# Row products by four blocks, scalings shared with ScalarE, and adjacency loads ahead of a store, in a four-layer graph network

## The reference, cut to what matters

```python
x = _layernorm(x + _L0_gnn_ref(x, ...))      # returns updated + x, so the norm sees 2x + updated
x = _layernorm(x + _L1_gnn_ref(x, ...))
x = _layernorm(x + _L2_gnn_ref(edge_index, x))
x = _layernorm(x + _L3_gnn_ref(x, ...))
```

```python
x_tangent = logmap0(x, c)                     # artanh(|x|) * x / |x|, a factor per row
support = x_tangent @ weight
hyp_bias = proj(expmap0(bias[None, :], c), c)
support = proj(mobius_add(support, hyp_bias, c), c)
agg = segment_sum(edge_weight[:, None] * support[col], row)
return proj(expmap0(agg, c), c)

def mobius_add(x, y, c):
    x2, y2, xy = sum(x * x), sum(y * y), sum(x * y)
    num = (1.0 + 2.0 * c * xy + c * y2) * x + (1.0 - c * x2) * y
    return num / maximum(1.0 + 2.0 * c * xy + c * c * x2 * y2, MIN_NORM)
# proj(x): x scaled down to norm 0.996 where its norm is larger
```

## Time and profile before

| | |
|---|---|
| median of three runs | 5073.99 us (5068.99 to 5074.60) |
| the profiled execution | 5076.37 us, its span 5074.6 us |
| busy: PE, PEld, DVE, ACT, POOL | 3733.3, 2726.1, 3254.3, 1313.6, 1977.1 us |
| accumulation | 2314 to 3121 us |
| first norm and row products, to the end of S | 3121 to 3235 us |
| weighted adjacency | 3235 to 3924 us |
| second norm | 3924 to 3973 us |

### The profile page before, as it was taken

How to read it: one execution, slowest core, us unless ns; L and a number is a source line. 1 busy time by engine, 2 the same in 40 slices (tenths; PEclk the granted TensorE clock), 3 DMA queues, 4 the chain that set the end, 5 groups by cost and what they waited for, 6 DMA issues and landing times. The chain is left out here.

```text
span 5074.6 us, 99492 instructions
## 1 busy us (share of the span) xinstructions
PE 3733.3 (74%) x38930; PEld 2726.1 (54%) x38930; DVE 3254.3 (64%) x4529; ACT 1313.6 (26%) x3164; POOL 1977.1 (39%) x2050
## 2 busy tenths in 40 slices
PE   4457755555555555555888886499998699989997
PEld 3345655555555555545777775255555244444444
DVE  7886898888888889875777766666666400230022
ACT  0015666555565555640000002100001100010000
POOL 0051277777776777745777773000000003000300
PEclk6558898988988889887999997799999899989998
DMA  9636889999999999997788785488885467656664
GB/s 314 225 103 223 274 301 342 337 340 342 342 338 334 338 343 347 339 247 236 228 230 232 226 230 121 183 304 305 304 305 203 152 204 227 198 165 202 212 191 140
DMA packets 710810, 1297.27 MB, mean 256 GB/s; under 512 B 367384, under 2 KB 512428, under 8 KB 701260
## 3 DMA queue, kind: packets, MB, share of 16 engines
q1 hardware_dynamic: 579516, 823.86, 49.9%
q10 hardware_dynamic: 60300, 314.88, 16.2%
q0 software_dynamic: 70576, 152.66, 11.7%
HBM read 814.90 MB, written 529.03 MB: 265 GB/s over the span
## 5 line engine op out<-in xcount | busy, mean ns | idle before, releaser
L1460 PE MATMUL psum<-big 128*128 128x98 bf16 x7936 | 925.7, 215 | 702.5 <-DVE big L1441 489.6
L1411 POOL DMA_INDIRECT big<-typed_msgs,big x1216 | 1150.1, 946 | 516.2 <-issue 330.7
L1460 PEld LDWEIGHTS psum<-big 128*128 128x128 bf16 x7936 | 789.7, 100 | 755.9 <-DVE big L1441 524.6
L2111 PE MATMUL psum<-big 128*128 128x512 bf16 (+1 forms) x4704 | 992.1, 373 | 82.3 <-DMA big<-adj 82.3
L1461 PE MATMUL psum<-big 128*128 128x49 bf16 x7936 | 911.5, 197 | 2.3 <-issue 2.3
L1462 PE MATMUL psum<-big 128*128 128x49 bf16 x7936 | 907.0, 190 | 0.1
L1462 PEld LDWEIGHTS psum<-big 128*128 128x128 bf16 x7936 | 838.0, 106 | 1.7 <-issue 1.6
L1461 PEld LDWEIGHTS psum<-big 128*128 128x128 bf16 x7936 | 794.5, 100 | 2.7 <-issue 2.7
L2111 PEld LDWEIGHTS psum<-big 128*128 128x128 bf16 x4704 | 460.3, 98 | 605.6 <-DMA big<-adj 82.8
L1696 PE MATMUL psum<-big 128*128 128x192 f32 x3648 | 647.5, 333 | 118.2 <-DMA big<-typed_msgs,big 98.0
L1921 PE MATMUL psum<-big 128*128 128x416 f32 x1984 | 655.4, 494 | 63.4 <-DVE big L1955 62.3
(11 more groups left out here) (320 smaller groups left out, 2753.2 us busy)
## 6 DMA issues: line engine op xcount, KB each, us to landing
wadj<-big ACTq DMA_DIRECT2D x248, 784.0 KB
big<-wadj SPq DMA_DIRECT2D x124, 1568.0 KB, 7.0
big<-adj SPq DMA_DIRECT2D x210, 896.0 KB, 4.8
big<-staged SPq DMA_DIRECT2D x304, 384.0 KB
staged<-big SPq DMA_DIRECT2D x60, 1920.0 KB
adj<-big ACTq DMA_DIRECT2D x62, 1568.0 KB
big<-edge_feats SPq DMA_DIRECT2D x456, 128.0 KB
edge_feats<-in_edge_attr SPq DMA_DIRECT2D x1, 51562.5 KB, 162.5
```

Of the source, the lines that this page charges most:

```text
L1411: pool.indirect_dma_start(out=sgot4[:, c, u, 0:D], out_offset=None, in_=typed_rows, in_offset=bass.IndirectOffsetOnAxis(ap=pairs4i[:, g, u ...
L1460: pe.matmul(to[:, 0:2 * NB], lo, hi_b[:, q, t, 0:2, 0:NB], start=True, stop=False)
L2111: last = pe.matmul(ps[c % 2][:, 0:len(blocks) * P], terms_[:, k, b * D:(b + 1) * D], ring_a[:, m % RA, 0:len(blocks), s * P:(s + 1) * P], ...
```

## The change

In the accumulation, the first 128 columns of each block of `acc` start as 2X in place of zero, the other 64 as zero. The pass L1734 is dropped, and the norm reads `acc` in place.

In the row products, ScalarE's copies of X are dropped: TensorE turns four blocks straight from X into one PSUM bank, ScalarE evicts the 512 columns at once, TensorE makes four products into one bank, and ScalarE evicts them at once. TensorE turns the next four blocks ahead of the products of the last. VectorE's sums stay per block, written out in place of a loop.

The norm of the result is computed from the sums at hand (|a s + p y|^2 = a^2 s^2 + 2 a p s y + p^2 y^2), and the factor of `proj` is folded into `a` and `part_y`. Then ScalarE scales blocks 0 to 39 by `a`, VectorE blocks 40 to 48, and VectorE adds the bias part block by block, waiting for ScalarE's block where it is one.

In the weighted adjacency stage the store of `support` is issued after the first four loads. The degree roots move from the second norm to VectorE's list between its last transpose and its last evictions. The squares behind the stage move into it: VectorE makes them block by block behind ScalarE's evictions, and ScalarE's part of them is dropped.

```diff
@@ accumulation, VectorE
-                dve.memset(acc, 0.0).then_inc(s_clear, 1)
+                dve.tensor_scalar(acc3[:, :, 0:D], X3, 2.0, None, ALU.mult).then_inc(s_clear, 1)
+                dve.memset(acc3[:, :, D:ACCW], 0.0).then_inc(s_clear, 1)
@@ first norm, VectorE
-                link(dve.scalar_tensor_tensor(h43, X3, 2.0, sums, ALU.mult, ALU.add))
...
-                layer_norm(dve, link, h43, chain.sqrt, logs)
+                layer_norm(dve, link, sums, chain.sqrt, logs)
...
-                        dve.wait_ge(s_S5, i * BB + (k + 1))
-                        at_least(dve, s_sum5, (i * BB + (k + 1 - BB)) * 2)
...
+                for b in range(NB):
+                    k = b % BB
+                    dve.wait_ge(s_S5, b // BB + 1)
+                    at_least(dve, s_sum5, (b + 1 - BB) * 2)
...
-                link(dve.tensor_tensor(S3, S3, along(a), ALU.mult))
-                link(dve.tensor_tensor(sq43, bias3, along(x2), ALU.mult))
-                link(dve.tensor_tensor(S3, S3, sq43, ALU.add))
-
-                sum_of_squares(dve, link, S3, sq43, den)
-                chain.sqrt(den, a)
-                link(dve.tensor_scalar(a, a, MIN_NORM, None, ALU.max))
-                link(dve.reciprocal(a, a))
-                link(dve.tensor_scalar(a, a, MAX_NORM, 1.0, ALU.mult, ALU.min))
-                link(dve.tensor_tensor(S3, S3, along(a), ALU.mult))
+                link(dve.tensor_tensor(sq, a, x2, ALU.mult))
+                link(dve.tensor_tensor(den, part_y, xy, ALU.mult))
+                link(dve.scalar_tensor_tensor(sq, den, 2.0, sq, ALU.mult, ALU.add))
+                link(dve.tensor_tensor(sq, sq, a, ALU.mult))
+                link(dve.tensor_tensor(den, part_y, part_y, ALU.mult))
+                link(dve.scalar_tensor_tensor(sq, den, y2, sq, ALU.mult, ALU.add))
+                link(dve.tensor_scalar(sq, sq, 0.0, None, ALU.max))
+                chain.sqrt(sq, den)
+                link(dve.tensor_scalar(den, den, MIN_NORM, None, ALU.max))
+                link(dve.reciprocal(den, den))
+                link(dve.tensor_scalar(den, den, MAX_NORM, 1.0, ALU.mult, ALU.min))
+                link(dve.tensor_tensor(a, a, hi, ALU.mult))
+                link(dve.tensor_tensor(a, a, den, ALU.mult))
+                dve.sem_inc(s_factor, 1)
+                link(dve.tensor_tensor(part_y, part_y, den, ALU.mult))
+                for b in range(SCALED, NB):
+                    made = dve.tensor_scalar(S3[:, b, :], S3[:, b, :], a[:, b:b + 1], None, ALU.mult)
+                link(made)
+                for b in range(NB):
+                    if b < SCALED:
+                        dve.wait_ge(s_scaled, b + 1)
+                    made = dve.scalar_tensor_tensor(S3[:, b, :], b1b[:, :], part_y[:, b:b + 1], S3[:, b, :], ALU.mult, ALU.add)
+                link(made)
@@ row products, ScalarE
-                    for k in range(n):
-                        at_least(act, s_xT5, i * BB + (k + 1 - BB))
-                        act.copy(xst4[k], X[:, bass.ds(i * (BB * D) + k * D, D)]).then_inc(s_xs5, 1)
...
+                def rows_out(j):
+                    b0, b1 = QUADS[j]
+                    act.wait_ge(s_o5, j + 1)
+                    act.copy(S[:, b0 * D:b1 * D], ps[BB + j % 4][:, 0:(b1 - b0) * D]).then_inc(s_S5, 1)
+
+                for j, (b0, b1) in enumerate(QUADS):
+                    act.wait_ge(s_xT5, j + 1)
+                    at_least(act, s_o5, j - 1)
+                    act.copy(xTs[:, j % 2, 0:(b1 - b0) * D], ps[j % 4][:, 0:(b1 - b0) * P]).then_inc(s_xTe5, 1)
+                    if j:
+                        rows_out(j - 1)
+                rows_out(len(QUADS) - 1)
                 chain.answer(act, before_products[0])
+                act.wait_ge(s_factor, 1)
+                for b in range(SCALED):
+                    act.activation(S3[:, b, :], S3[:, b, :], ACT.Identity, scale=sm(6)[:, b:b + 1]).then_inc(s_scaled, 1)
@@ row products, TensorE
+                def products(j):
+                    b0, b1 = QUADS[j]
+                    pe.wait_ge(s_xTe5, j + 1)
+                    at_least(pe, s_S5, j - 3)
+                    for i in range(b1 - b0):
+                        last = pe.matmul(ps[BB + j % 4][:, i * D:(i + 1) * D], xTs[:, j % 2, i * D:(i + 1) * D], w1s[:, :],
+                                         start=True, stop=True)
+                    last.then_inc(s_o5, 1)
+
+                for j, (b0, b1) in enumerate(QUADS):
+                    at_least(pe, s_xTe5, j - 3)
+                    for b in range(b0, b1):
+                        last = pe.transpose(ps[j % 4][:, (b - b0) * P:(b - b0 + 1) * P], X[:, b * D:(b + 1) * D], ident)
+                    last.then_inc(s_xT5, 1)
+                    if j:
+                        products(j - 1)
+                products(len(QUADS) - 1)
@@ weighted adjacency, SP
-                sp.dma_start(support.rearrange("(b p) f -> p b f", p=P), S3).then_inc(s_support, 16)
                 for s in range(S2):
                     for m, j in enumerate(blocks7):
                         n = s * GB + m
+                        if n == RW:
+                            sp.dma_start(support.rearrange("(b p) f -> p b f", p=P), S3).then_inc(s_support, 16)
                         at_least(sp, s_turned7, n - RW + 1)
@@ weighted adjacency, VectorE, behind the last transpose; the roots leave the second norm
+                link(dve.tensor_scalar(dinv, outdeg, 1.0, None, ALU.add))
+                chain.sqrt(dinv, dinv)
+                link(dve.reciprocal(dinv, dinv))
+                link(dve.tensor_scalar(degn, indeg, 1.0, None, ALU.max))
+                chain.sqrt(degn, degn)
+                link(dve.reciprocal(degn, degn))
                 take(1)
+                for b in range(NB):
+                    dve.wait_ge(s_agg7, b // QUAD + 1)
+                    row = agg_st[:, b * D:(b + 1) * D]
+                    made = dve.scalar_tensor_tensor(sq83[:, b, :], row, 1.0, row, ALU.mult, ALU.mult, accum_out=sm(3)[:, b:b + 1])
+                link(made)
@@ second norm, VectorE
-                sum_of_squares(dve, link, g, sq83, raw)
```

More of the change, by code:

```diff
@@ L129 @@
 BB = 4
-SHARE = 18
 NORM_SHARE = 19
@@ L659, in wide @@
             return v.rearrange("p (b f) -> p b f", b=NB)
-        def sum_of_squares(dve, link, h3, sq3, to):
-            asked = chain.squares(h3, sq3, to)
-            link(dve.tensor_tensor(sq3[:, SHARE:, :], h3[:, SHARE:, :], h3[:, SHARE:, :], ALU.mult))
-            link(dve.tensor_reduce(out=to[:, SHARE:], in_=sq3[:, SHARE:, :], axis=AX.X, op=ALU.add))
-            dve.wait_ge(chain.did, asked)
         def layer_norm(dve, link, h3, ask_sqrt, before_x=lambda: None, counted=False):
@@ L721, in sqrt @@
                 self.func(ACT.Sqrt, i, o)
-            def squares(self, h3, sq3, to):
-                self.k += 1
-                self.jobs.append((self.k, None, h3, sq3, to))
-                self.dve.sem_inc(self.ask, 1)
-                return self.k
             def rows(self, h3, x3, scale, shift_):
@@ L744, in answer @@
                         made.then_inc(self.did, 1)
-                    elif f is not None:
+                    else:
                         act.activation(o, i, f).then_inc(self.did, 1)
-                    else:
-                        for b in range(SHARE):
-                            made = act.activation(o[:, b, :], i[:, b, :], ACT.Square, accum_out=to[:, b:b + 1])
-                        made.then_inc(self.did, 1)
         s_turn = sem("s_turn")
@@ L1702, in build @@
         sq4, S = (cut(i * NB * D, NB * D)[0] for i in range(2))
-        h4, rest4 = cut(2 * NB * D, NB * D)
+        e_turned, at = cut(2 * NB * D, NB * P)
+        e_turned = e_turned[0:FE, :]
+        xTs, at = cut(at, 2 * BB * D)
+        xTs = xTs.rearrange("p (k x) -> p k x", k=2)
         assert NB * ACCW <= 2 * NB * D
-        h43, S3, sq43 = wide(h4), wide(S), wide(sq4)
-        def staged(n, width):
-            nonlocal rest4
-            c, rest4 = cut(rest4, n * width)
-            return [c[:, k * width:(k + 1) * width] for k in range(n)]
-        xst4, xTs4 = staged(BB, D), staged(BB, D)
-        e_turned = staged(1, NB * P)[0][0:FE, :]
+        S3 = wide(S)
         EB = 4
@@ L1719, in build @@
         s_x1 = sem("s_x1")
-        s_xs5 = sem("s_xs5")
+        s_scaled = sem("s_scaled")
+        s_factor = sem("s_factor")
+        SCALED = 40
+        QUADS = [(b, min(b + BB, NB)) for b in range(0, NB, BB)]
         s_xT5 = sem("s_xT5")
@@ L1863, in build @@
         turned = turned.rearrange("p (k x) -> p k x", k=RT)
+        top = big_words - 2 * NB * D
+        sq8 = cut(top, NB * D)[0]
+        h8 = cut(top + NB * D, NB * D)[0]
+        sq83, h83 = wide(sq8), wide(h8)
+        assert top >= 2 * NB * D
+        dinv = small[:, 12 * NB:13 * NB]
+        degn = small[:, 13 * NB:14 * NB]
         agg_st = agg7
@@ L1930, in _ @@
                                  ident).then_inc(s_turn7, 1)
-            @block.scalar
```

(11 more changed lines are left out.)

77 lines of the change are left out of this document (28 added, 49 removed).

## The result

The changed kernel takes 5021.52 us (median of four runs, 5020.33 to 5023.03), the kernel before beside it 5074.3 us (5068.99 to 5075.5): a ratio of 0.9898, 95% interval 0.9881 to 0.9915. The profiled execution took 5023.03 us with a span of 5021.3, 53.3 us less than the span before.

The account below looks back on a forecast made before the run. A serial chain through VectorE, ScalarE and TensorE, then TensorE in the weighted adjacency stage, was taken as the bound. 6.7 + 15.9 + 17.9 + 6.1 + 2.1 + 4.3 = 53.0 us off 5073.99 gave 5021 us, range 5011 to 5036.

Parts of the forecast that it names:

- Zeroing, 0: Start of the accumulation: writing 2X and zeros in place of one memset changes nothing, 0 us, range -2 to +2.
- The sum before the norm, 6.7: Before the first norm: the 6.69 us instruction forming 2X plus the sums goes, saving 6.7 us.
- Row products, 15.9: Row products: groups of four blocks without copies run at VectorE's pace, 27.4 us in place of 43.3, saving 15.9.
- Factors and scaling, 17.9: Scale, bias and norm of the support: 22.5 us in place of 40.4, saving 17.9 us.
- Loads ahead of the store, 6.1: Weighted adjacency stage: TensorE opens 10.4 us earlier but stands some 4 us before the fifth block, saving 6.1 us.
- the slower rival: Weighted stage: TensorE's clock falls to 1.2 GHz at the stand and stays; at twelve slow blocks 5084 us; chance 0.03.
- Degree roots, 2.1: End of the weighted stage: the roots leave the chain, hidden under VectorE's 7.02 us wait for TensorE, saving 2.1 us.
- Squares behind the stage, 4.3: End of the weighted stage: squares made block by block during ScalarE's evictions, ending at 3928.3 in place of 3932.6, saving 4.3 us.
- The stages outside: Stages outside the changed ones: none should move by more than 2 us, else the prediction counts itself wrong.
- the late clock: Row products: clock stays low; gain 4 us less if late, 9 if never, 5025 to 5030 us; chance 0.15.
- the argument from TensorE not standing: Row products: clock rises early since TensorE has 2.7 us of work a group at low clock, ScalarE needing 1.
- The per-block hand-over: Scaling of the support: ScalarE at 0.39 or VectorE at 0.35 us a block sets the end, 5024 to 5025; chance 0.08.

Follow-up runs that it names:

- three_passes: Changed kernel with the factors applied in three whole-width VectorE passes over S instead of the shared block scaling and bias steps; 5037.09 us, ratio 0.9913.
- shared_squares: Changed kernel with ScalarE making the squares of every fourth block (12 of 49) in the row products; 5871.12 us, ratio 0.992.
- products_by_block: Changed kernel with the row products put back block by block, with ScalarE's copies, small evictions and loops; 5044.09 us, ratio 0.9924.
- even_scale: Changed kernel with the doubling of X split into two instructions, 48 blocks and one; 5815.38 us, ratio 0.9903.
- even_scale_2: Changed kernel with the doubling as 48 blocks and one, the store ahead of the 13th load, and 43 blocks scaled by ScalarE; 5860.23 us, ratio 0.991.
- all_four: Changed kernel with doubling as 48 blocks and one, store ahead of the 13th load, 43 blocks on ScalarE, and ScalarE sharing squares; 5866.01 us, ratio 0.9913.
- store_first: Changed kernel with the support store issued ahead of the loads, as before the change; 5032.62 us, ratio 0.99.
- store_late: Changed kernel with the support store issued ahead of the 13th load in place of the 5th; 5024.53 us, ratio 0.9887.
- the first group: First of three groups of four follow-up kernels, each run beside the kernel before, which took 5077.93 us in this one and 5874.64 and 5919.74 in the others.

## Why the prediction was right

5021 us were forecast, 5021.5 measured, and the sum of 53.0 us stands against 53.3 in the spans. The mechanism held in each stage, but an agreement to half a microsecond is luck: the products gave 1.8 us more than forecast, the loads 1.7 less, scaling and squares 0.9 more, and the stages outside took 0.8 back. By its steps:

- **Zeroing, 0**: 0.06 us, but not by the reckoning, so this is luck too. I had weighed an instruction at half its time, by the Trainium skill (VectorE: DVE Perf Modes, the perf-mode tier table), against 6.69 us, and left open which. It was 6.69 us at 49 blocks; the other value exists, at 48. By that the stage should have opened 1.4 us later, but the first instruction started 2.0 us sooner than the memset had, which I hadn't seen in the rows.
- **The sum before the norm, 6.7**: 6.7, and 6.7 again when it was put back.
- **Row products, 15.9**: 17.7. The first sum came 4.6 us after the first turn, not 5.2, and the clock rose just as VectorE finished its small work, so nothing was lost to it where I had put 1.2 us. The pace of 1.7 us a group was right: 20.9 us for 49 blocks.
- **Factors and scaling, 17.9**: 18.4. ScalarE took 0.29 us a block as taken, VectorE 0.264 for the bias, as taken too; the nine scalings took 0.206 against 0.264 each, half a microsecond in all.
- **Loads ahead of the store, 6.1**: 4.4, the step that was mis-sized. The stand of 4 us and its place (37.4 us, forecast 37.7) were right. The fall of the clock had been named only as the slower rival, at ten blocks or more; a short one inside the stand's own block was missing from the sum. The nine executions with the store behind the fourth load show both outcomes. In seven of them, with stands of 3.7 to 5.3 us, the clock fell to 1.2 GHz within 1.4 us of the stand's end. In five it stayed there for 3.4 us, and from the fifth block's start to the eighth transpose were 12.6 us; in three_passes and shared_squares, which had the longest stands (4.8 and 5.3 us), it stayed for 6.8 us, and the same stretch took 14.0 and 13.7. The stage took 675.9 to 677.7 us. In two (products_by_block, even_scale), with stands of 1.5 and 3.4 us, the clock stayed at 2.4 GHz; the stretch took 10.9 us in both, the stage 673.6 and 674.3. So a fall costs 1.7 to 3.1 us, and without one the term is 6.0 to 6.7, about as forecast. The falls went with the longer stands, and behind the 15th block's stands of 1.6 and 1.8 us in even_scale_2 and all_four there was none either; these are too few for a bound. The row of the stand and the window behind it in even_scale, beside those of the changed kernel above:

```profile
3917.77 12.47 PE L1933 MATMUL psum<-big 128*128 128x416 f32 x37 [3.40 <-DVE big L1959]
3917.78:3921.78 4.00, 4.00 (x12) 2.38 (x13) 3.04 (x1) 0.00 (x0) 2.84 (x3) 1.00 1.02 401
```

- **Degree roots, 2.1**: hidden, with 5.13 us of VectorE's wait left. **Squares behind the stage, 4.3**: 4.7.
- **The stages outside**: -1.1, +2.7 and -0.8 us. The +2.7 is beyond the 2 us that I had allowed, and by the prediction's own words a sign of being wrong. Five executions of kernels with the doubling took 807.6 to 812.0 us in the accumulation, the one of before 807.3. One line of the trace shows what bounds it (GpSimd's gathers in the changed kernel: idle time before them, and how often):

```profile
L1586 POOL DMA_INDIRECT big<-typed_msgs,big x608: 938/945/1461, 2313.5 to 3108.0; - x152
  issue: 182.4, 597
  PE psum L1679: 9.5, 10
```

608 gathers follow each other at 1.31 us from start to start, and stand on TensorE for 9.5 of 795 us. So TensorE's opening can give little there, whatever the zeroing costs, and the length is that of GpSimd's own series. The 2.7 us lie in the gathers themselves: GpSimd was busy with the 608 for 604.0 us, before for 601.2, with the same idle time to half a microsecond; with the same doubling they took 600.3 (store_first) to 603.8 us (store_late) in the first group. So most of the 2.7 us is the gathers' spread. That the change adds a microsecond of its own is neither shown nor excluded: the runs meant to separate it met the slower DMA, in which the gathers stand 127 to 190 us and the length wanders by more than that.

Of the rivals the late clock did not come. With groups it came early every time: in all twelve executions that have them it rose 3.4 to 6.1 us after the first turn, and those without shared squares took 25.4 to 26.3 us for the products, the longest where it rose last. The block-by-block code, in which TensorE stands, met it at 11 us in one kernel and at 23 in the other. That fits the argument from TensorE not standing, but no run shows that this is what brings the clock. The per-block hand-over was within 0.003 us of the forecast; and the fall of the clock, the rival on the other side, came in small: 1.7 us, not 63.

## What to carry to other kernels

Group the hand-over between engines before thinking about removing the copies in it: here the four-block groups were worth some 12 us, 14 with the earlier clock, and the copies 0.6. When a transfer is moved back in a queue, place it where the ring behind it is full, and price the stand it leaves with the clock that falls after it; behind the fourth load was too early, and ahead of the thirteenth it cost nothing in one execution and 2 to 3 us in two. And look at the outermost counts of an elementwise instruction: 48 blocks took half the time of 49, from a contiguous source to a target in rows.

## What the runs showed of the hardware that I had not expected

- A doubling of 49 x 128 elements took 6.69 us, one of 48 x 128 3.36 us, and a gather issued beside the second 3.50 to 3.51 us in place of 0.94, in three kernels.
- The memset at the head of a stage started 2.0 us later than a tensor_scalar at the same place, in both kernels that had it.
- The same program ran 16 to 17% longer in two of the three groups, with the DMA share at 0.75 in place of 1.00 in its gather stages and the stages inside SBUF unchanged.
- Behind the stand before the fifth block the clock fell in seven executions, with stands of 3.7 to 5.3 us, and not in two, with 1.5 and 3.4 us; a fall lasted 3.4 or 6.8 us and cost 1.7 to 3.1 us.
